# A slot-by-slot graph attention kernel: twelve more tiles part their slots into high and low neighbours

## The reference

```
Wh = x @ W
e = (Wh @ a_src)[:, None] + (Wh @ a_dst)[None, :]
e = where(e > 0, e, slope * e)
attention = softmax(where(adj > 0, e, MINUS_A_LOT), axis=1)
x = layernorm(x + elu(attention @ Wh))
```

## Time and profile before

| | |
|---|---|
| median of 3 runs | 655.91 us (655.78 to 656.47) |
| profiled execution | 651.55 us, its span 649.8 us |
| busy, share of the span | PE 61%, VectorE (DVE) 62%, ScalarE (ACT) 52%, POOL 47% |
| gathers on POOL | 292 (73 in each of four layers), 288.0 us busy |
| mean granted TensorE clock | 0.797 |

### The profile page before, as it was taken

How to read it: one execution, slowest core, us unless ns; L and a number is a source line. 1 busy time by engine, 2 the same in 40 slices (tenths; PEclk the granted TensorE clock), 3 DMA queues, 4 the chain that set the end, 5 groups by cost and what they waited for, 6 DMA issues and landing times.

```text
span 649.8 us, 10378 instructions
## 1 busy us (share of the span) xinstructions
PE 395.6 (61%) x3269; PEld 338.9 (52%) x3281; DVE 404.8 (62%) x1899; ACT 335.0 (52%) x753; POOL 305.0 (47%) x323
## 2 busy tenths in 40 slices
PE   2255445336675579763286866538787754887861
PEld 1244334225564468642176766426687743786851
DVE  2214689933558988985066799616568851556985
ACT  3377787385567866861072244616334551542444
POOL 0000065561061346808777770477777057777600
PEclk9999999999999999995598665559856555795555
DMA  8998999966378712001221220121222022222200
GB/s 307 399 415 311 430 414 408 389 201 224 129 244 312 261 13 35 18 26 27 27 28 27 36 35 19 41 35 29 28 36 34 22 43 36 29 29 36 42 17 29
DMA packets 20546, 84.84 MB, mean 131 GB/s; under 512 B 6083, under 2 KB 11462, under 8 KB 16262
## 3 DMA queue, kind: packets, MB, share of 16 engines
q1 hardware_dynamic: 10102, 73.15, 28.6%
q0 software_dynamic: 9344, 9.89, 11.7%
q10 hardware_dynamic: 1040, 1.08, 0.5%
HBM read 78.72 MB, written 5.37 MB: 129 GB/s over the span
## 4 chain that ended last, share of the span: by engine, by line
DVE 32%; PE 18%; POOL 15%; issue 10%; ACT 9%; DMA 2%; DVEq 0%; ACTq 0%
POOL xg L632 15%; PE bank L975 5%; ACT arena L1084 4%; PE bank L821 3%; PE bank L923 3%; DVE sooner L1780 3%; PE bank L806 2%; DVE nbr L1402 2%; DVE stats L1881 1%; ACT score L1110 1%; DVE score L1586 1%; PE bank L903 1%; DVE xg L1833 1%; DMA xg<-table,index 1%; PE bank L938 1%
## 5 line engine op out<-in xcount | busy, mean ns | idle before, releaser
L632 POOL DMA_INDIRECT xg<-table,index x292 | 288.0, 986 | 309.3 <-DMA table<-wh 145.0
L1084 ACT ACTIVATE arena<-arena,half 128x4096 bf16<-128x4096 int32 x31 | 114.5, 3700 | 19.2 <-DMA arena<-in_adj_t 18.7
L975 PE MATMUL bank<-xg,arena 128*128 128x65 f32 x486 | 93.5, 374 | 0.9 <-DVE xg L1833 0.9
L975 PEld LDWEIGHTS bank<-xg,arena 128*128 128x128 f32 x486 | 91.8, 291 | 2.1 <-issue 1.2
L938 PE MATMUL bank<-packed,xg 128*128 128x128 f32 x219 | 47.8, 351 | 51.6 <-DMA xg<-table,index 44.1
L1381 DVE MAX8 top<-bank 128x8 f32<-128x256 f32 x31 | 13.3, 430 | 83.6 <-PE bank L723 83.6
L938 PEld LDWEIGHTS bank<-packed,xg 128*128 128x128 f32 x219 | 33.6, 184 | 55.5 <-DMA xg<-table,index 46.2
L1780 DVE CUSTOM_DVE_ANT_0 sooner<-bank,arena 128x256 bf16<-128x256 f32 (+3 forms) x114 | 46.0, 439 | 24.4 <-PE bank L938 23.8
L1762 DVE CUSTOM_DVE_ANT_0 score<-bank,score 128x512 f32<-128x512 f32 x24 | 16.6, 691 | 51.6 <-ACT score L1174 51.3
L1174 ACT ACTIVATE score<-bank,sloped_own 128x512 f32<-128x512 f32 x24 | 16.5, 687 | 60.0 <-PE bank L891 60.0
L1235 ACT ACTIVATE x<-res,shift,stat 128x64 f32<-128x64 f32 x96 | 34.4, 431 | 21.5 <-DVE shift L1897 21.5
(11 more groups left out here) (195 smaller groups left out, 889.0 us busy)
## 6 DMA issues: line engine op xcount, KB each, us to landing
arena<-in_adj_t SPq DMA_DIRECT2D x31, 2048.0 KB, 11.1
xg<-table,index POOLq DMA_INDIRECT x292, 2.8
table<-wh SPq DMA_DIRECT2D x24, 132.0 KB, 1.9
arena<-in_adj SPq DMA_DIRECT2D x1, 2048.0 KB, 12.8
table<-wh ACTq DMA_DIRECT2D x1, 1056.0 KB, 26.3
x<-in_x SPq DMA_DIRECT2D x1, 1024.0 KB, 14.9
out_x<-x SPq DMA_DIRECT2D x8, 128.0 KB, 2.0
packed<-in_c_packed SPq DMA_DIRECT2D x1, 308.0 KB
```

What stands on the lines that cost most here:

```text
L632: pool.indirect_dma_start(out=xg[:, c, :], out_offset=None, in_=table[l][0:rows, :], in_offset=bass.IndirectOffsetOnAxis(ap=index[:, c:c + ...
L975: t = nc.tensor.matmul(agg_ps[g % 2][:, at:at + F + 1], one_hot[:, place:place + P], xg[:, c, 0:F + 1], start=(c == FIRST[k]), stop=(c == ...
L1084: nc.scalar.activation(masks[:, t % 2, :], arena[:, t % 3, :], ACT.Sign, bias=half[:, :]).then_inc(mask_made, 1)
```

## The change

Tiles 8 to 19 become parted tiles as tiles 1 to 7 are, each with one chunk set aside for its high neighbours.

```
-PARTED = 8
-HIGH_TO = [0, 2, 2, 1, 1, 2, 1, 1]
+PARTED = 20
+HIGH_TO = [0, 2, 2, 1, 1, 2, 1, 1] + [1] * 12
 EARLY = [FIRST[k] + c for k in range(PARTED) for c in range(HIGH_TO[k], CHUNKS[k]) if TILES_OF_CHUNK[FIRST[k] + c] == [k]]
```

## The result

The changed kernel takes 720.47 us (718.16 to 720.64, 3 runs) against 655.91: 1.097 times the time before (95% interval 1.094 to 1.101), 64.6 us more. The profiled execution is 720.64 us with a span of 718.8.

What follows compares the result with a forecast made beforehand. The prediction took work following other work to bound the kernel, each layer's rounds being started by the 19th gather. Terms 52.4 - 2 + 6 - 2 = +54.4 us on the median of 655.91 gave 710 us, range 695 to 725.

Steps and rivals of the forecast that it cites:

- Gathers, number and pace: POOL's gathers: 73 in each layer before and after, the last one still the 73rd; 0 us.
- Their order: POOL's queue: first strip ready at the 33rd gather instead of the 19th, 17.5 us later in three layers; +52.4 us.
- What is absorbed: PE's waits for later strips' gathers in layers 1 and 2 vanish; -2 us, bounds 0 and 6.7.
- List making: First layer, mainly VectorE: three more batches of parted tiles, partly covered by idle time; +6 us, bounds 0 and 12.6.
- PE's clock: PE behind the first strip: another start may change layer 2's or 3's full-clock time; -2 us, bounds -7 and +4.
- A (catching up): PE between first and last strip: rounds catch up with POOL, 656 to 662 us; chance 0.06 in part, 0.02 wholly.
- B (an idle queue filled): POOL before whole-table gathers: early gathers fill idle time, up to 17.5 us less each layer, 604 us; chance 0.01.
- C: Tile 9's high slots pass their limit, sending every layer down the dense path, over 2000 us; chance 0.03.

Runs made afterwards that it cites:

- e2: Kernel before with its old lists and masks, but POOL issuing gathers in the changed kernel's order: 710.4 us, 1.082 times the time before.
- e7: Changed kernel with only the first 24 of its 31 early gathers early, first strip complete at the 26th gather: 690.4 us.
- e5: Changed kernel with all strips' stages nine rounds later, so the dense tile's rounds come first: 679.3 us.
- e10: Kernel before, unchanged, profiled once more: 655.3 us, the profiled execution 654.4.
- e1: Changed kernel's parted lists for all twelve tiles, but POOL's gather order of before (17 early): 665.5 us, 1.018 times the time before.
- e4: Kernel before with only the first 10 of its 17 early gathers early: 652.2 us, 0.993 of the time before.
- e6: Kernel before with the strips' stages four rounds later: 648.5 us, 0.988 of the time before.
- e8: Kernel before with the strips' stages nine rounds later: 660.0 us, median of four runs (660.2, 647.0, 659.8, 663.6).
- e11: Changed kernel with 240, 170 and 170 identity transposes on PE before its wait for the first strip in layers 1, 2, 3: 719.8 us.
- e9: Kernel before with 10 early gathers and the strips four rounds later: 652.5 us, 0.995 of the time before.

## Why the prediction was right

It said 710 us (695 to 725), slower with 0.98; measured 720.5. The sum was +54.4 us and the result is +64.6. The mechanism and its size were right; the three small terms all erred to the same side, so the time came out near the upper bound of 725.

1. *Gathers, number and pace, 0:* as said; 288.9 us busy against 288.0.
2. *Their order, +52.4:* right, with 52.6 in the trace. The waits for the first strips were forecast at about 36, 27 and 26 us and are 36.4, 27.3 and 26.3; from start to first strip it is 17.6, 17.5 and 17.5 us more. e2 shows that the place in the queue alone costs 54.9 us, e7 that it goes place by place, and e5 that the dense tile's work, held behind the wait, could have run in it, as point 2 had it. "Nothing covers this" was right for this order of stages only.
3. *What is absorbed, -2:* the gather waits of the later strips did vanish, but the stretches did not get shorter: 67.7 to 73.7 us against 68.4 to 73.5 in e10. There layers 1 and 2 have no later gather wait to absorb, and layer 3, which the prediction had at no wait, has 6.1 us. The waits come and go between executions while the stretch keeps its length within the same few us. The term should have been 0, as its own argument on layer 1 (another engine holds the rounds) suggested for all three.
4. *List making, +6:* too low. The first layer is longer by 7.2 us against the first profile and by 8.0 against the second, and e1 costs 10.0 us in its median of four runs, which vary by 6. The marks cost about what was summed (the last mark starts 3.8 us behind the first instead of 0.9, so 2.9 more against 3.2); the part taken to be covered by VectorE's idle time was too large. VectorE's waits for PE from 190 us on are still 2.0 us in the changed kernel (2.3 in the earlier trace rows), so they took next to nothing:

```profile
  PE bank L723: 2.0, 2
```

   The cover between 135 and 190 us was real: those waits fell from 34.7 to 30.6 us, near one batch's 4.2. That leaves 12.6 - 4.1 - 0.3 = 8.2 us, beside the measured 8.0.
5. *PE's clock, -2:* wrong in sign. It took layer 2 of the one profile at hand as the rule and layer 3 as the exception. That execution was unusually good in layers 1 and 2: e10 and the changed kernel both start layer 1 at 0.74 and 0.66, not 0.86 and 1.00. In layer 3 the stretch did get shorter by 0.8 us; in layers 1 and 2 it got longer by 3.5 and 4.7. The prediction said that this execution was 4.4 us under the median and moved the sum to the median, but did not ask which of its rows were too short.
6. *The rivals:* A (catching up) is refuted, since no strip behind the first waits for a gather and the stretch is 68 to 74 us. B (an idle queue filled) is refuted by the rows of POOL, and e4 shows from the other side that with 10 early gathers POOL does wait, if only for 2.0 and 2.7 us. C did not happen; the later layers ran slot by slot.

Against the sum: 52.6 from the order and 8.0 from the list work, as measured by stage, are 60.6 of 64.6. The rest, some 4 us, has its place in layer 2's stretch (3.1 us more than in e10) and behind the last strip (2.8 us more), and lies within what executions of one kernel differ by (653.2 to 657.2 in e10); how much of it is the change's stays open.

## What to carry to other kernels

Before moving work ahead of a wait, look whether the queue ever stands at that wait; if it doesn't, an item moved forward only pushes back what it passes, and what counts is the place of the item that the next engine needs first. In a pipeline whose stages are written in a fixed order, a late first input costs its whole delay even when the last input comes no later, unless independent work is put ahead of its wait. How much is best was not settled here: nine rounds suited waits of 26 to 36 us (e5), four suited waits of 9 to 19 (e6), and nine there gave no usable answer (e8). And where a profiled execution is shorter than the median, find the rows that are short before a term is built on them.

## What was not expected of the hardware

The granted clock behind the first strip was the same after two different spells of 36 us: one idle throughout at 0.50 (the changed kernel), one with 26.5 us of transposes, nearly all at 1.00, and then 9.9 us idle (e11). Both then had 0.74 to 0.76 and 0.66 in the next two 10 us stretches. And executions of one unchanged kernel fall into groups by the clock: of 23 executions of the kernel before that were timed beside e9 and e10, five took 652.2 to 653.0 us with a mean granted clock of 0.794 to 0.799, and the other eighteen took 654.8 to 660.4 us with 0.770 to 0.784. The two profiled ones differ in the same way: 70.2 us from first to last strip of layer 1 with the clock at 0.86 and 1.00 behind the first strip, 73.5 us with 0.74 and 0.66. What decides which of the two an execution gets, no run here shows.
